# Edge codes loaded in evenly divisible pieces, statistics quads one group ahead, a look-up before a barrier, and waits moved off GpSimd's queue

## The reference

```python
x = _layernorm(x + gat_two_layers(x, src, dst, ...))      # 4 heads, softmax over the edges of a destination
x = _layernorm(x + mean_over_edges(x @ L1_W.T) + L1_b)
x = _layernorm(x + edge_mlp_sum_mean_max(x, edge_attr))   # relu(concat(x[dst], attr) @ W1) @ W2
x = _layernorm(x + gat_one_head(x, ...))
```

## Time and profile before

| | |
|---|---|
| runs | 2214.3, 2215.8, 2217.61 us; median 2215.8 |
| profiled execution | 2213.13 us, span from first to last instruction 2211.1 us |
| PE / DVE / ACT / POOL busy | 80% / 72% / 50% / 53% of the span |
| mean granted clock of TensorE | 0.72 of full speed |

### The profile page before, as it was taken

One profiled execution on the slowest core, in us unless ns is written; L12 is line 12 of the kernel. 1 busy time (PEld: TensorE's weight loads), 2 busy tenths in 40 slices (PEclk: granted clock), 3 DMA queues, 4 the chain that ended last, 5 costly groups with the idle time before them and its releaser, 6 DMA issues. The chain is left out here.

```text
span 2211.1 us, 31785 instructions
## 1 busy us (share of the span) xinstructions
PE 1767.0 (80%) x7816; PEld 1200.7 (54%) x7816; DVE 1602.7 (72%) x5809; ACT 1102.3 (50%) x3760; POOL 1180.9 (53%) x1242
## 2 busy tenths in 40 slices
PE   1998989996558899079777886999788999599992
PEld 1898888885543333069655553777662222155551
DVE  4766554655978998089778986999766666798882
ACT  0332323231485576045456765777577877433331
POOL 5777777773007777512277772000007777267776
PEclk9686766666698898555589987999995555575555
DMA  5664555551038787145588875555749999423440
GB/s 89 193 191 148 163 151 163 152 157 56 21 120 260 211 250 220 35 133 196 177 209 269 241 229 180 165 175 178 188 144 339 373 311 315 147 89 105 139 127 19
DMA packets 279786, 388.48 MB, mean 176 GB/s; under 512 B 95678, under 2 KB 124338, under 8 KB 279348
## 3 DMA queue, kind: packets, MB, share of 16 engines
q1 hardware_dynamic: 228668, 302.59, 42.7%
q0 software_dynamic: 37632, 67.06, 11.8%
q10 hardware_dynamic: 13304, 16.80, 2.3%
HBM read 236.61 MB, written 153.52 MB: 176 GB/s over the span
## 5 line engine op out<-in xcount | busy, mean ns | idle before, releaser
L701 POOL DMA_INDIRECT ring<-x_t,idx x280 | 268.2, 958 | 409.4 <-SPq L324 324.7
L701 POOL DMA_INDIRECT ring<-in_x_dram,idx x392 | 375.8, 959 | 139.9 <-issue 116.5
L701 POOL DMA_INDIRECT big<-hidden_e,idx x196 | 198.2, 1011 | 192.3 <-DVE idx L1649 133.1
L707 POOL DMA_INDIRECT out_dram<-outr,idx x196 | 196.8, 1004 | 106.4 <-issue 58.5
L763 ACT ACTIVATE outr<-z,rn 128x128 f32<-128x128 f32 x392 | 161.5, 482 | 171.7 <-DMA out_dram<-outr,idx 128.5
L2235 PE MATMUL bank<-DB,z 20*128 20x512 f32 x196 | 201.3, 1128 | 23.2 <-DVE outr L1623 7.4
L1186 DVE BATCH_NORM_STATS2 stats<-ring 128x6 f32<-128x128 f32 x196 | 42.8, 280 | 169.5 <-DMA ring<-in_x_dram,idx 151.8
L1122 ACT ACTIVATE msg<-bank 128x512 f32<-128x512 f32 x98 | 58.5, 597 | 191.3 <-PE bank L1054 191.3
L1080 PEld LDWEIGHTS bank<-bT,msg 128*128 128x128 f32 x784 | 135.8, 260 | 1.0 <-ACT msg L1122 0.9
L1080 PE MATMUL bank<-bT,msg 128*128 128x4 f32 x784 | 134.9, 295 | 0.7 <-ACT msg L1122 0.7
L1379 DVE TENSOR_TENSOR_SCAN G<-cont,G,bank 65x512 f32<-65x512 uint8 (+1 forms) x96 | 121.0, 1260 | 10.5 <-PE bank L1886 10.1
(11 more groups left out here) (464 smaller groups left out, 4928.7 us busy)
## 6 DMA issues: line engine op xcount, KB each, us to landing
hT<-in_x_dram SPq DMA_DIRECT2D x194, 256.0 KB
x_t<-outr SPq DMA_DIRECT2D x147, 256.0 KB
ring<-x_t SPq DMA_DIRECT2D x147, 256.0 KB, 3.2
xsrc_e<-ring SPq DMA_DIRECT2D x49, 256.0 KB, 2.6
xd_e<-ring ACTq DMA_DIRECT2D x49, 256.0 KB
ring<-xsrc_e SPq DMA_DIRECT2D x49, 256.0 KB, 4.0
x_t<-xT SPq DMA_DIRECT2D x49, 256.0 KB
ring<-xd_e SPq DMA_DIRECT2D x49, 256.0 KB, 2.6
```

Source lines behind the costliest of these rows:

```text
L701: nc.gpsimd.indirect_dma_start(to(c), None, table, bass.IndirectOffsetOnAxis(ap=idx[:, kind, (g + 1) * GT + c:(g + 1) * GT + c + 1].bitcas ...
L707: nc.gpsimd.indirect_dma_start(table, bass.IndirectOffsetOnAxis(ap=idx[:, kind, (g + 1) * GT + c:(g + 1) * GT + c + 1].bitcast(U32), axis= ...
```

## The change

1. **Loads.** Each of the four code loads is cut in 96 rows, one row, and the rest; `dst` and `src` themselves go first, on SP, with a semaphore of their own. The loads of single numbers are gone: TensorE turns the rows of `src` and `dst` first of all (`turn_row`), VectorE copies them (`row_in`), and POOL waits for these two (`torow` 2).
2. **Stage a.** The two quads of group g + 1 are turned before the rows of group g, through two banks in turn and four column buffers; the last group's rows are turned after everything else. The products share a bank with `project`'s results, and ScalarE copies them out instead of VectorE.
3. **Look-up.** The code broadcasts start in stage b, and `hot(0)`, `hot(1)`, `look(0)`, `pick(0)`, `hid(0)` stand at the end of b, ahead of the barrier.
4. **Waits.** After c, and after h, SP waits for the landings instead of POOL; after c POOL passes the barrier by `sem_inc` without a drain.
5. **Stage e** gathers into 8 slots (4 in `ring`, 4 in `big`); the slots after the first 4 wait until `x3_indices` has read `big`.

```diff
-        def arrive(eng):
-            eng.drain().then_inc(phase, 1)
+        def arrive(eng, drained=True):
+            if drained:
+                eng.drain().then_inc(phase, 1)
+            else:
+                eng.sem_inc(phase, 1)
...
-            (e_src[0:FULL, :], src[0:FULL * CH].rearrange("(q c) -> q c", c=CH)),
...
+        EVEN = FULL - FULL % 16
+        def code_loads(to, frm, shift):
+            return [
+                (to[0:EVEN, :], frm[shift:EVEN * CH + shift].rearrange("(q c) -> q c", c=CH)),
+                (to[EVEN:FULL, :], frm[EVEN * CH + shift:FULL * CH + shift].rearrange("(q c) -> q c", c=CH)),
+                (to[FULL:FULL + 1, 0:REST - shift], rowof(frm[FULL * CH + shift:E])),
+            ]
+        edges = code_loads(e_dst, dst, 0) + code_loads(e_src, src, 0)
...
-            if half:
-                for n, frm in ((SRC, src), (DST, dst)):
-                    eng.dma_start(idx[:, n, GT:GT + RING * GT], frm[0:RING * GE].rearrange("(c p) -> p c", p=P), ...)
...
-                if g == 0:
-                    pool.wait_ge(S("idx0"), 32)
-                if g == RING:
+                if g == 0:
                     pool.wait_ge(S("torow"), 2)
...
+            for g in range(NG - 1):
+                hist_add(g)
+                stat_turn(2 * g + 2)
+                stat_turn(2 * g + 3)
+                turn(g)
+                products(2 * g)
+                products(2 * g + 1)
                 if g:
                     project(g - 1)
...
+            hot, pick, hid = lookups(v)
+            hot(0)
+            hot(1)
+            pick(0)
+            hid(0)
...
-            for j in range(RING):
-                wait(pool, f"c_in{j}", GT * 16 * (BODIES + (j == 0)))
...
+            for j in range(RING):
+                wait(sp, f"c_in{j}", GT * 16 * (BODIES + (j == 0)))
...
-            barrier(pool)
+            barrier(pool, False)
...
+        def e_rows(g):
+            k = g % OQ
+            return ring[:, k, 0] if k < RING else part(k, GE).rearrange("p (t f) -> p t f", f=F)
```

More of the change, by code:

```diff
@@ L303, in shared @@
                 return name, 0
-            start = 0
+            start = GT * 16 * len(range(RING + int(slot), NG, 2 * RING)) if kind == "sc" else 0
             for t, per in users.items():
@@ L504, in prep_tensor @@
             pe.wait_ge(S("prep_dve"), PREP_DVE["tomake"])
-            for m in range(5):
-                if m % 2 == 0 and m:
+            for m in range(2, 5):
+                if m % 2 == 0:
                     pe.wait_ge(S("torow"), m)
[L508 to L511, removed]
+                turn_row(m)
             pe.wait_ge(S("torow"), 5)
@@ L1399, in halves, with look_bank, look, codes @@
             return P if j < GB else HF
+        def look_bank(t):
+            return bank[(0, 1, 5, 6)[t] if t < GT else t % 5][:, 0:HI]
+        def look(pe, g):
+            need(pe, "look_oh", g + 1)
+            for c in range(GT):
+                t = GT * g + c
+                need(pe, "look_pick", t - 4)
+                lhs = oht[g % 3][:, c * P:(c + 1) * P]
+                nc.tensor.matmul(look_bank(t), lhs, table[:, 0, :], start=True, stop=False)
+                nc.tensor.matmul(look_bank(t), lhs, table[:, 1, :], start=False, stop=True).then_inc(S("look_mm"), 1)
+        def codes(sp, g):
+            need(sp, "look_oh", g - 3)
+            sp.dma_start(slb[g % 4], srclo_d[g * GE:(g + 1) * GE].partition_broadcast(P)) \
+                .then_inc(S(f"slb{g % 4}"), 16)
+        def lookups(v):
+            def hot(n):
+                v.wait_ge(S(f"slb{n % 4}"), 16 * (n // 4 + 1))
+                need(v, "look_mm", GT * (n - 2))
+                v.tensor_scalar(oht[n % 3], slb[n % 4], pcol[:], None, ALU.is_equal).then_inc(S("look_oh"), 1)
+            def pick(n):
+                for c in range(GT):
+                    t = GT * n + c
+                    need(v, "look_mm", t + 1)
+                    v.scalar_tensor_tensor(picked[:, c, :], iota[:], shi[:, t:t + 1], look_bank(t),
+                                           ALU.is_equal, ALU.mult, accum_out=found[:, t:t + 1]) \
+                        .then_inc(S("look_pick"), 1)
+            def hid(n):
+                need(v, "look_pick", GT * (n + 1))
+                need(v, "c_hid", n)
+                v.tensor_scalar(hidt[:], found[:, four(n)], 0.0, hpad[:], ALU.is_equal, ALU.mult) \
+                    .then_inc(S("dve_chain"), 1)
+                Chain.done += 1
+                v.wait_ge(S("dve_chain"), Chain.done)
+                v.scalar_tensor_tensor(idx[:, HID, GT * (n + 1):GT * (n + 2)], hidt[:], -1.0, found[:, four(n)],
+                                       ALU.add, ALU.add).then_inc(S("c_hid"), 1)
+            return hot, pick, hid
         def b_vector(v):
@@ L1530, in b_sync @@
                 sp.dma_start(W2d[n * HF:(n + 1) * HF, n * HW:(n + 1) * HW], W2x[:]).then_inc(S("b_w2"), 16)
+            sp.wait_ge(S("srclo_out"), 16)
+            for n in range(RING):
+                codes(sp, n)
             for j in range(GA):
@@ L1666, in c_vector @@
             extra[38] = scaled
-            for n in range(LEAD):
-                hot(n)
-                if n:
-                    pick(n - 1)
-                    hid(n - 1)
+            hot(2)
+            pick(1)
+            hid(1)
             for g in range(NG):
@@ L1732, in store @@
                 sp.dma_start(edge_row(x1s_e, g), outf[:, g % RING, :]).then_inc(S(f"c_out{g % RING}"), 16)
-            for g in range(4):
-                codes(g)
-                if g < 2:
-                    load(g)
+            load(0)
+            load(1)
             for g in range(NG + 2):
                 if g + 4 < NG:
-                    codes(g + 4)
+                    codes(sp, g + 4)
                 if g + 2 < NG:
@@ L1837, in attend_pool @@
             at_tiles(step)
-            for j in range(RING):
-                wait(pool, f"{tag}_sc{j}", GT * 16 * (BODIES + (j == 0)))
         def linear_sync(sp, tag, table, to, rev, used, more=None, also=()):
@@ L2391, in _ @@
             linear_sync(sp, "h", x3_e, None, True, "_z", xs_e)
+            for j in range(RING):
+                wait(sp, f"h_sc{j}", GT * 16 * (BODIES + (j == 0)))
             barrier(sp)
```

195 lines of the change are left out of this document (91 added, 104 removed).

## The result

| | before | changed |
|---|---|---|
| median of three runs | 2215.8 us | 2184.66 us (2178.54 to 2187.21) |
| profiled execution | 2213.13 us | 2178.54 us, span 2176.8 us |

The ratio is 0.9849, with a 95% interval of 0.9826 to 0.9872: 1.5% faster, 31 us in the medians and 34.6 us between the profiled executions. Forecast were 34 us and 2182 us. Run again, the changed kernel took 2186.84 us against 2219.01 (ratio 0.9852, 0.9832 to 0.9872).

The account below looks back on a forecast made before the run. POOL's gathers were taken to bound stages a and e, with idle stretches between stages; 12.2 + 3.0 + 2.5 + 7.7 + 7.6 + 1.2 = 34.2 us off gave 2178.9 profiled, 2182 median, range 2172 to 2198.

Parts of the forecast that it names:

- first gather earlier: Start of stage a: POOL's first gather at 10.0 us instead of 22.22, saving 12.2 us.
- slot wait in a gone: Stage a: POOL no longer waits for a ring slot because prep ends earlier, saving 3.0 us.
- tail of a: End of stage a: work moved ahead of the last gathered rows saves 2.5 us, bounds -2 and 5.5.
- early look-up: From b to c: codes fetched and first look-up done before the barrier, saving 7.7 us, bounds 5.5 and 9.
- no drain after c: End of c: only the last rows' landing, 2.1 us, remains of 9.7, saving 7.6 us.
- end of h: Kernel's end: POOL's drain starts without first waiting for the landing, saving 1.2 us, between 0 and 2.1.
- stage e: Stage e: more slots remove at most 1.2 us that nobody waits for, priced at 0.
- rival 1: Prep and stage a: weights or POOL's slots stay late, losing 15.2 us of the first two terms, 2197 us; 15%.
- the late first gather: Start of a, bound: slower issues and slowest landing put the first gather at 13.3 us, saving 8.9 us.
- the best of the drain term: End of c, upper bound: landing of 1.5 us, below a's, saves 8.3 us.
- The middle of a: Stage a's steady state: POOL's 10.0 us a group rules, so the new order is priced at nothing.
- rival 3: Stage a: TensorE becomes the bound at a clock of 0.50 throughout, kernel slower at 2266 us; 5%.

Follow-up runs that it names:

- 2: Changed kernel with three code loads as 97-row pieces again, new load order kept, no single-number loads: 2200.66 us, 13.8 slower than the changed kernel.
- 4: Kernel before with only its three 97-row code loads cut in 96 rows and one: 2207.26 us against 2220.41, ratio 0.9931.
- 5: Changed kernel with the last group's rows in stage a turned ahead of its products, as in the old tail: 2190.0 us, 3.2 slower in the median.
- 12: Changed kernel without POOL's last drain, stage a in old order for 48 groups, last group's rows turned last: 2187.17 us, ratio 0.9865.
- 11: Changed kernel with POOL also passing the very last barrier without a drain, SP still waiting for every scatter: 2187.98 us, ratio 0.9867.
- 6: Changed kernel with wait for landings and drain after stage c back on POOL: 2196.26 us, ratio 0.9886.

## Why the prediction was right, and where not

| term | forecast | profile | by undoing it |
|---|---|---|---|
| first gather earlier | 12.2 | 12.7 | 13.8 |
| slot wait in a gone | 3.0 | 3.0, less 1.6 in slower gathers | not undone: gone in 2 and 4 too |
| tail of a | 2.5 | -0.1 | 3.2 (tail alone), -2.2 (whole order), with intervals that overlap |
| early look-up | 7.7 | 6.5 | 6.4 profile, 4 in time |
| no drain after c | 7.6 | 7.6 | 7.5 |
| end of h | 1.2 | 1.2 | 1.2 profile |
| stage e | 0 | 1.7 | 0 |

All in us; the last column is how much slower the undone version was, a minus where it was faster.

**The start.** The sum was right, and prep's end at 36.2 lay well before the 40.2 from which rival 1 decides, so that rival fell. Two bounds beside it were added up a little wrong, without effect on the forecast: the late first gather is 13.0 (3.5 + 3.8 + 3.3 + 0.7 + 1.7), not 13.3, and the best of the drain term 8.2, not 8.3. The prediction's reading of the earlier trace rows was incomplete. It laid the late weights on ScalarE's load of single numbers, which held its queue to 17.4. That load had to come together with the 97 rows. The kernel before with even pieces keeps it and shows it at 1.56 us, the last weights issued at 15.41 and prep's end at 36.6; the changed kernel with 97-row pieces doesn't have it, and there the last weights are issued at 12.20 and don't hold VectorE. The first cast and the first gather need no such partner: with 97 rows and no load of single numbers they still come at 20.16 and 22.76. So the 97 rows alone caused VectorE's first idle time and were enough to hold POOL, and the two loads together caused the wait for the weights. The front of this document has each of the four loads cut in 96 rows, one row and the rest, and the prediction speaks of one piece of 97 rows; there were three, and the fourth load had 96 from the start.

The rule of the Trainium skill that stood beside the rows (DMA: Bandwidth & Descriptors, "Why a DMA increments its semaphore by 16 and not by 1") is what both runs bear out in direction, 11.5 us in the one and 13.3 in the other, and the DMA share of 0.07 fits one engine out of sixteen. The same page's "Rules for kernel authors", which would join small transfers, points the wrong way here: three more transfers, 13 us less.

**The tail of a** is the step that failed. I priced it by the order of the rows behind the last turn, as if what moves ahead of the turn were done while the last rows land. But in neither kernel does TensorE wait for them: the turn at 521.63 in the earlier trace rows has no idle time in brackets, and neither has the one at 510.85. A step moved from behind that turn to ahead of it then only makes the turn later, 4.8 us after the issue instead of 1.4. The order gains where the engine would have waited, as in 5, where it had waited 2.49 us. Here are the 17.3 us ahead of POOL's last issue, first before, then changed, with the columns of the earlier trace rows:

```profile
502.89:520.19 17.30, 14.30 (x96) 13.11 (x94) 6.82 (x44) 5.21 (x16) 13.18 (x14) 0.79 0.38 115
```

```profile
488.80:506.10 17.30, 17.30 (x107) 15.41 (x107) 6.80 (x46) 5.45 (x17) 13.21 (x14) 0.70 0.37 115
```

The 3.0 us idle before are one wait, for the rows of the group before the last, at 511.77; the changed kernel has none, so TensorE had already fallen behind there.

There is a second difference, the clock. These are the tails, from the last issue to the end of a, before, changed, 4 and 5:

```profile
520.23:532.89 12.66, 11.01 (x66) 10.37 (x65) 2.60 (x16) 3.61 (x12) 0.01 (x1) 0.63 0.08 26
506.08:518.80 12.72, 10.29 (x48) 9.80 (x47) 2.06 (x11) 2.60 (x12) 0.01 (x1) 0.50 0.08 26
508.24:524.00 15.76, 13.41 (x64) 12.91 (x62) 2.71 (x16) 3.61 (x12) 0.00 (x0) 0.50 0.06 21
507.47:522.65 15.18, 11.15 (x52) 11.06 (x52) 2.06 (x11) 2.49 (x12) 0.00 (x0) 0.50 0.07 22
```

The kernel before had its tail at a granted clock of 0.63, the changed one at 0.50, which is the lower of TensorE's two levels (1.2 GHz). At 0.50 the tail with the last rows turned first took 15.8 us (4) and 15.2 (5), and the nine profiles with the dense order and the new tail have 12.7 to 15.5, the middle one 13.6, all at 0.50. That is some 2 us less at the same clock, so it may be that the order gave most of its 2.5 us and the lower clock took them. It isn't shown: no profile has the new tail at a higher clock, and 12, with the new tail at 0.50, took 16.3 (it turns its last two quads there as well). Why the clock differs stays open. It doesn't follow from how busy TensorE was: of the two stretches of 17.3 us the busier one has the lower clock, so the rule of the Trainium skill that the prediction weighed (TensorE: Matmul & The Clock Gate, Part 1) is not borne out by them either; and 11 has 14.98 us busy at 0.79 in that stretch and then a tail of 14.5 at 0.50.

The middle of a was priced rightly: first to last issue takes 495.7 to 498.0 us in all fourteen profiles, whatever the order, and rival 3 (TensorE as the bound) shows itself only in that lateness at the end.

**The look-up** was mis-sized by 1.2 us. Index to gather had been 0.8 us in the earlier trace rows (666.03 to 666.81), and I let the gather follow the barrier by 0.1; it follows its index by 0.8 again. The other part is TensorE: b's last sixteen products took 4.17 us at a granted clock of 0.50 (before, two bursts of eight took 1.14 and 1.07 at 1.00), and VectorE waited 2.33 for the first look-up's product, where I had 0.9. In 6, where TensorE's clock stood at 0.99 up to the first gather, that gather came after 6.3 us instead of 6.6.

**The drain** and **the end of h** came as worked out, the last rows of c having landed 2.2 us after their issue (forecast 2.1). The sum of the terms in the profile is 12.7 + 1.4 - 0.1 + 6.5 + 7.6 + 1.2 = 29.3 us; the two profiled executions differ by 34.6. The other 5.3 lie in c's gathers (257.6 us from first to last before, 255.0 after), in e (269.9 to 268.2) and in g (258.4 to 257.5), with a tenth or two in f and h. The second profile of the changed kernel has 269.9 for e and 289.8 for f (before 287.7), so I take these for differences between executions, and the medians' 31 to 32 us for the change. The forecast of 34 was high by about the tail and the look-up's error.

## What to carry to other kernels

Look at the row count of each load on the path before at its place in the queue: cutting 97 rows into 96 and one gave 13 of the 32 us, and a blocked queue shows first as someone else's long issue. A step moved ahead of a wait is worth the idle time that stands there, not the length of the step: look first whether the row behind the wait has any idle time, and at what clock it runs. Before taking a wait or drain off one engine, see whether what it waits for is waited for again further on.

## What the runs showed of the hardware

Loads of 97 rows moved 24 GB/s between 5 and 8 us with a DMA share of 0.07, and held later issues: with two of them on SP's queue, a one-row load behind the second took 5.6 us to issue before and 7.1 in 2, against 0.2 to 0.3 with even pieces. On ScalarE's queue, with one of them ahead, a one-row load took 3.6 us and a load of 2,048 single numbers 9.28, against 0.3 and 1.56 with even pieces; in 2, without loads of single numbers, no issue there took over 0.7. POOL's drain behind indirect DMAs costs 7.5 us beyond their landing when it starts after it (9.7 us from the last issue in c, 2.2 without it), 8.1 from the last issue when it starts at once, and leaving it out at the program's end gains nothing (9.1 without it).
